# A linear-attention and mixture-of-experts kernel: quads of tiles, chunks of 64 tokens and transposed experts

## The chip, the cores and the metric

The kernel runs on one core of one Trainium2 chip. The metric is the device time of one execution in microseconds (us), as the median of several runs.

## What is computed

The input is 8 sequences of 1024 tokens with 128 features, float32.

```python
x = L0_attn_x
xn = _layernorm(x, axis=-1)
x = x + attention(xn) + experts(xn)
# attention: 16 heads of 8; k is layer-normed in each head; causal, linear (no softmax)
scores = jnp.where(causal, einsum('bthd,bshd->bhts', q_c, k_c), 0.0)
intra = einsum('bhts,bshd->bthd', scores, v_c); S = S + einsum('bthd,bthe->bhde', v_c, k_c)
# experts: 8, one for each token, the one with the largest affinity
assign = jnp.argmax(xn @ centroids.T, axis=1)
h = relu(einsum('etd,efd->etf', layernorm(xn) * ln_g + ln_b, w1) + b1)
y = xn + einsum('etf,edf->etd', h, w2) + b2
out = a * y + (1.0 - a) * xn          # a = sigmoid(xn . centroid)
```

The reference carries the state S from chunk to chunk of 64 tokens. Because nothing in the attention is nonlinear, any chunk length gives the same sum.

## The kernel before

A tile is 128 tokens; there are 64 tiles. A **quad** is four tiles of four sequences at the same place; there are 16 quads, and the quads of the two halves of the batch alternate. Every engine has a program of its own, in which the order of its work is written out by hand; semaphores hold the engines together. The program has three stages, one after the other.

- **Preparation** (`chunk`, 8 times; lines 1053 on for TensorE): tokens are loaded, layer-normed and transposed; affinities are computed; each expert's weights are loaded and transposed, with `ln_g` folded in; POOL adds the normed tokens to the residual and clears the slots in HBM. Then VectorE ranks all tokens by expert at once (lines 855 to 908).
- **Quads** (`quad`, 16 times). For each tile, `qk_trans` (L1096, L1098) transposes q and k, which were split into float16 parts; `scores` (L1108) makes, for each of four groups `g` of 32 rows, four products of 32 x 128 by 128 columns in float16. ScalarE copies half of the scores out of PSUM (L538) and POOL masks them (L343), VectorE masks the other half (L767). `weighted` (L1126) multiplies the scores by the values: 16 float32 products for each tile, with 128 x 32 weights and 128 columns. `inter` (L1118) adds the part of the state, `output` (L1134) applies W_o, `project` (L1065) makes q, k and v, `state_step` (L1139) updates the state. POOL also scatters each token's row to its slot in HBM (`scatter_rows`, L354).
- **Experts** (72 slots of 128 tokens in rounds of 8): `load_slots` reads a slot, `se_trans` (L1224) transposes it, `se_up` makes three products of 512 columns (L1232 to L1234, fp32r parts), VectorE adds the bias (L944), `se_hidden` (L1240) transposes the hidden layer, ScalarE applies relu (L605), `se_down` (L1248) makes four float32 products, VectorE adds b2 and scales (L952, L955), and POOL scatters the result into the output with an add (`scatter_out`, L410).

On TensorE a float32 product stands in the trace as two loads and two MATMUL records, a transpose or a float16 product as one of each.

## Time and profile before

| | |
|---|---|
| median of 3 runs | 767.69 us (765.97 to 768.08) |
| span of the profiled execution | 763.3 us; the median is 4.4 us above it |
| preparation, quads, experts | 85.5, 514.5, 163.3 us of the span |
| TensorE busy | 719.8 us (94%) |
| DVE, ACT, POOL busy | 387.7, 283.2, 329.9 us |

The page has a busy time for each engine, the span in 40 slices, the DMA queues, the chain of work that ended last and the costliest groups of instructions. The profiled execution has no other time of its own than its span. "L1126" is line 1126 of the kernel. PE is TensorE, PEld its weight loads, DVE is VectorE, ACT ScalarE, POOL GpSimd. Ends of matmuls are modelled, so the step from one start to the next tells the pace.

### The profile page before, as it was taken

Reading aid. Unit: us, or ns where it says so; the run is one execution under the profiler, and the core shown is the slowest. Engines: PE = TensorE matmul, PEld = TensorE weight load, DVE = VectorE, ACT = ScalarE, POOL = GpSimd, SP = SyncE. Lnnn points to the kernel's source line nnn. Section 1 sums busy time; section 2 is a strip of 40 time slices with the busy share of each in tenths; the row PEclk is TensorE's granted clock in tenths of the full one; section 3 lists DMA queues with packets and bytes.
Section 4 is the critical chain, followed back from the end, with each engine's and each line's share of the span. In section 5 each row is a group of like instructions: output and inputs, shape, how many; then the busy total and the mean of one; then the engine's idle time right before and its main releaser. Section 6 shows DMA issues by size and latency. Waiting matters only on the chain.

```text
span 763.3 us, 18096 instructions
## 1 busy us (share of the span) xinstructions
PE 719.8 (94%) x5828; PEld 568.7 (75%) x5830; DVE 387.7 (51%) x1080; ACT 283.2 (37%) x586; POOL 329.9 (43%) x361
## 2 busy tenths in 40 slices
PE   1896899999999999999999999999999899999994
PEld 1443677777777777777777777777777798899994
DVE  5978444343434434443344433444443577667773
ACT  1786233333333323323233233332433343434341
POOL 3553353333333333343333333333321277776776
PEclk9999699999999999999999999999999899999998
DMA  9791000000000000000000000000001154444451
GB/s 236 210 257 37 15 16 23 12 22 27 8 21 11 21 20 12 21 7 24 7 24 21 7 24 7 24 21 8 26 17 31 32 65 61 55 61 59 61 62 11
DMA packets 49807, 32.08 MB, mean 42 GB/s; under 512 B 8296, under 2 KB 46440, under 8 KB 49776
## 3 DMA queue, kind: packets, MB, share of 16 engines
q0 software_dynamic: 13840, 13.93, 10.7%
q1 hardware_dynamic: 32816, 17.73, 8.9%
q10 hardware_dynamic: 3120, 0.01, 0.2%
q8 instruction: 18, 0.29, 0.2%
q14 instruction: 13, 0.11, 0.1%
HBM read 14.07 MB, written 18.10 MB: 42 GB/s over the span
## 4 chain that ended last, share of the span: by engine, by line
PE 89%; DVE 3%; DMA 2%; issue 2%; SPq 1%; POOL 1%; ACT 1%; POOLq 0%; DVEq 0%; ACTq 0%
PE bank L1126 33%; PE bank L1108 11%; PE bank L1248 7%; PE bank L1065 7%; PE bank L1240 4%; PE bank L1118 4%; PE bank L1134 4%; PE bank L1096 3%; PE bank L1232 2%; PE bank L1234 2%; DMA resid<-in_L_attn_x_dram 2%; PE bank L1233 2%; PE bank L1139 2%; PE bank L1098 2%; PE bank L1060 1%
## 5 line engine op out<-in xcount | busy, mean ns | idle before, releaser
L1126 PE MATMUL bank<-pr,vz 128*32 128x128 f32 x2048 | 271.9, 276 | 0.0
L1126 PEld LDWEIGHTS bank<-pr,vz 128*32 128x32 f32 x2048 | 203.0, 110 | 27.9 <-issue 0.2
L343 POOL TENSOR_SCALAR_AFFINE_SELECT pr<-pr 128x512 f32<-128x512 f32 x128 | 81.4, 636 | 308.7 <-ACT pr L538 308.7
L767 DVE TENSOR_TENSOR pr<-bank,causal 128x512 f32<-128x512 f32 x128 | 88.0, 688 | 164.3 <-PE bank L1108 164.2
L410 POOL DMA_INDIRECT out_dram<-qs,idxe x72 | 112.3, 1559 | 58.7 <-DVE qs L955 32.3
L538 ACT ACTIVATE pr<-bank 128x512 f32<-128x512 f32 x128 | 76.3, 596 | 125.9 <-PE bank L1108 125.9
L1108 PE MATMUL bank<-qqt,kkt 32*128 32x128 f16 x1024 | 101.0, 218 | 1.6 <-DVE kkt L762 1.6
L762 DVE COPY kkt<-bank 128x512 f16<-128x512 f16 x64 | 27.2, 425 | 119.9 <-PE bank L1098 116.0
L1108 PEld LDWEIGHTS bank<-qqt,kkt 32*128 32x128 f16 x1024 | 56.9, 93 | 36.3 <-issue 15.3
L1248 PE MATMUL bank<-w2t,pr 128*128 x576 | 76.0, 275 | 0.0
L1248 PEld LDWEIGHTS bank<-w2t,pr 128*128 128x128 f32 x576 | 70.0, 192 | 6.4
L543 ACT ACTIVATE y<-bank 128x128 f32<-128x128 f32 x64 | 17.8, 277 | 152.3 <-PE bank L1126 150.0
L354 POOL DMA_INDIRECT slots_d<-xq,idxq x64 | 64.0, 999 | 22.3 <-POOL idxq L349 13.0
L944 DVE SCALAR_TENSOR_TENSOR pr<-bank,xs,b1b 128x512 f32<-128x512 f32 x72 | 54.1, 751 | 34.7 <-PE bank L1234 12.5
L605 ACT ACTIVATE pr<-bank 128x512 f32<-128x512 f32 x72 | 43.1, 598 | 72.3 <-PE bank L1240 48.7
L1065 PE MATMUL bank<-wqkv,xt 128*128 128x128 f32 x384 | 56.1, 290 | 0.7 <-ACT xt L501 0.7
L1065 PEld LDWEIGHTS bank<-wqkv,xt 128*128 128x128 f32 x384 | 47.2, 194 | 10.2 <-issue 9.1
L1240 PE MATMUL bank<-ident,pr 128*128 128x128 f32 x288 | 43.7, 275 | 0.0
L1096 PE MATMUL bank<-identh,qs 128*128 128x128 f16 x256 | 36.9, 224 | 5.1 <-DVE ks L757 5.1
L533 ACT ACTIVATE qqt<-bank 128x512 f16<-128x512 f16 x64 | 38.0, 593 | 8.0 <-PE bank L1098 7.7
L1232 PE MATMUL bank<-w1h,xse 128*128 x72 | 35.4, 491 | 2.3 <-DVE xse L938 2.0
L1096 PEld LDWEIGHTS bank<-identh,qs 128*128 128x128 f16 x256 | 23.7, 98 | 17.8 <-issue 17.8
(169 smaller groups left out, 931.0 us busy)
## 6 DMA issues: line engine op xcount, KB each, us to landing
slots_d<-zrow POOLq DMA_DIRECT2D x8, 594.0 KB, 6.6
xs<-slots_d SPq DMA_DIRECT2D x72, 66.0 KB
resid<-in_L_attn_x_dram SPq DMA_DIRECT2D x8, 512.0 KB, 6.6
out_dram<-res SPq DMA_DIRECT2D x16, 256.0 KB
state<-in_L_ffn_w_dram SPq DMA_DIRECT2D x8, 256.0 KB
res<-in_L_ffn_w_dram SPq DMA_DIRECT2D x8, 256.0 KB
out_dram<-qs,idxe POOLq DMA_INDIRECT x72
slots_d<-xq,idxq POOLq DMA_INDIRECT x64, 2.3
```

Source lines behind the costliest of these rows:

```text
L343: pool.affine_select(out=pr_v[:, g, :, :], in_=pr_v[:, g, :, :], compare_op=ALU.is_ge, fill=0.0, base=0, pattern=[[0, J], [1, P]], channel ...
L354: pool.indirect_dma_start(slots_d, bass.IndirectOffsetOnAxis(ap=idxq[:, half, i:i + 1], axis=0), xq[:, half, i, :], None, bounds_check=NS ...
L410: pool.indirect_dma_start(out_rows, bass.IndirectOffsetOnAxis(ap=idxe[:, a:a + 1].bitcast(U32), axis=0), ye[:, a, :], None, bounds_check=N ...
L538: nc.scalar.activation(pr[:, g, :], SC[0][:, :], ACT.Copy).then_inc(s("sc_even"), 1)
L767: nc.vector.tensor_tensor(pr_v[:, g, :, :], SC[1][:, :].rearrange("p (j t) -> p j t", j=J), bcast(causal[:, :], 1, J), ALU.mult)\
L944: nc.vector.scalar_tensor_tensor(out=hb[:, a % 2, :], in0=banks[a % 2][:, :], scalar=xs[:, a, D:D + 1], in1=b1b[:, e, :], op0=ALU.mult, op ...
L1065: last = mm(bank[:, i * P:(i + 1) * P], xt[:, i, :], wqkv[:, col:col + D], start=True, stop=True)
L1096: nc.tensor.transpose(qb16[:, j, :], qv, identh[:, :])
L1108: last = mm(SC[g % 2][:, j * P:(j + 1) * P], kkt[32 * g:32 * (g + 1), i % 2, j, :], qqt[32 * g:32 * (g + 1), i % 2, j, :], start=True, sto ...
L1126: last = mm(YB[32 * g:32 * (g + 1), 0:P], vz[:, i % 2, j, 32 * g:32 * (g + 1)], pr[:, g, j * P:(j + 1) * P], start=False, stop=(j == J - 1))
L1240: last = nc.tensor.transpose(banks[2 + a % 2][:, c * P:(c + 1) * P], hb[:, a % 2, c * P:(c + 1) * P], ident[:, :])
L1248: last = mm(banks[4 + a % 2][:, 0:D], ht[:, a % 2, c * P:(c + 1) * P], w2t[:, e, c, :], start=(c == 0), stop=(c == FC - 1))
```

## The change

Nearly every function is written anew, so the diff is cut to what the prediction speaks of. In words:

- **Chunks of 64.** Each tile is two chunks (`CH = 64`), with a state in the middle (`smid`). Scores beyond a chunk are not computed. A half-quad `h` is two tiles. `scores(h)` makes 32 float32 products with 32 rows, 64 columns of weights and 128 moving columns; successive ones lie on the four row groups, then on the other half of the columns. `products(h)` makes 32 with 128 rows, 32 columns of weights and 64 moving columns, successive ones on the four column groups. Transposes of q and k in float16 parts are gone: q and k are projected already transposed, with one product of 512 columns each, and ScalarE spreads q over masked copies (`q_expand`, four for each quad).
- **Masks.** VectorE masks the scores of three banks in one instruction of 1536 elements (of all four, 2048, from half-quad 18 on); ScalarE copies and POOL masks the fourth.
- **Layer norm, routing, ranking and scatters** run beside the quads, in four batches of 16 tiles. Scatters go straight from `rows`. Slots lie by expert at fixed places in HBM, so only the tails are cleared.
- **Experts' weights** are loaded and transposed in quads 7 to 14, on TensorE in the place of the token transposes.
- **Experts.** 71 slots. The hidden layer is computed transposed (four float32 products of 128 columns, relu with the bias on ScalarE), so that its transposes and the fp32r parts are gone. VectorE copies each slot's weights, 1024 elements, to one of three buffers. All is written out; no loop is left.

```diff
+    CH = 64
+    NC = P // CH
+    PAIRS = J // 2
...
-    def scores(m, i, g):
-        if g == 0:
-            pe.wait_ge(s("qq_sb"), m + 1)
-            pe.wait_ge(s("kk_sb"), m + 1)
-        reach(pe, s("pr_odd" if g % 2 else "sc_even"), 2 * m + g // 2)
-        for j in range(J):
-            last = mm(SC[g % 2][:, j * P:(j + 1) * P], kkt[32 * g:32 * (g + 1), i % 2, j, :],
-                      qqt[32 * g:32 * (g + 1), i % 2, j, :], start=True, stop=True)
-        last.then_inc(s("sc_ps"), 1)
...
-    def weighted(m, i, par, g):
-        if g == 0:
-            pe.wait_ge(s("vz_ready"), m + 1)
-        pe.wait_ge(s("pr_odd" if g % 2 else "pr_even"), 2 * m + g // 2 + 1)
-        for j in range(J):
-            last = mm(YB[32 * g:32 * (g + 1), 0:P], vz[:, i % 2, j, 32 * g:32 * (g + 1)],
-                      pr[:, g, j * P:(j + 1) * P], start=False, stop=(j == J - 1))
-        last.then_inc(s("av_ps"), 1)
...
+    def scores(h):
+        n = h // 2
+        if h % 2 == 0:
+            pe.wait_ge(s("kT_sb"), n + 1)
+            pe.wait_ge(s("qx_sb"), n + 1)
+        reach(pe, s("se_sb"), min(h, ROUTED))
+        reach(pe, s("so_sb"), h)
+        for b in range(PAIR):
+            i = h % 2 * PAIR + b
+            for c in range(NC):
+                tok = slice(i * P + CH * c, i * P + CH * (c + 1))
+                at = b * TW + c * PAIRS * CH
+                for up in range(2):
+                    for g in range(G):
+                        r = slice(SW * g, SW * (g + 1))
+                        last = mm(SC[g][CH * up:CH * (up + 1), at:at + PAIRS * CH],
+                                  kT[r, n % 2, tok], qx[r, n % 2, i, 2 * up:2 * up + 2, CH * c:CH * (c + 1)],
+                                  start=True, stop=True)
+        last.then_inc(s("sc_ps"), 1)
...
+    def products(h):
+        n = h // 2
+        half = n % 2
+        if h % 2 == 0:
...
+            i = h % 2 * PAIR + b
+            if b and h == NH - 1:
+                pe.wait_ge(s("so_sb"), NH + 1)
+            for c in range(NC):
+                for p in range(PAIRS):
+                    for g in range(G):
+                        k = b * TW + (c * PAIRS + p) * CH
+                        last = mm(Y[half][SW * g:SW * (g + 1), i * P + CH * c:i * P + CH * (c + 1)],
+                                  vz[:, half, c, i, g, p, :], pr[:, h % 2, g, k:k + CH],
+                                  start=(n < 2 and i == 0 and c == 0 and p == 0),
+                                  stop=(i == HALF - 1 and c == NC - 1 and p == PAIRS - 1))
+        last.then_inc(s("av_ps"), 1)
...
+            for a in range(P // GW):
+                for c, bank in ((0, Y[n % 2]), (1, FA))[:2 if n < NQ - 2 else 1]:
+                    r, k = slice(CH * c, CH * (c + 1)), slice(i * D + GW * a, i * D + GW * (a + 1))
+                    last = mm(bank[GW * a:GW * (a + 1), i * GW:(i + 1) * GW], kn[r, n % 2, k], vp[r, k], start=True,
+                              stop=True)
+        last.then_inc(s("ds_ps"), 1)
...
+    def q_project(n):
...
+        mm(FA[:, :], wqkv[:, 0:D], xT[:, HALF * n:HALF * (n + 1), :].rearrange("p i t -> p (i t)"), start=True,
+           stop=True).then_inc(s("q_ps"), 1)
...
+    for h in range(NH):
+        n = h // 2
+        more = n + 1 < NQ
+        norm = n + 1 < NCH
+        scores(h)
+        if h % 2 == 0:
+            if more:
+                kT_project(n + 1)
+            state_step(n)
+            if h:
+                products(h - 1)
+            inter_first(n)
+            if more:
+                k_transpose(n + 1)
+            if n and out_early(n):
+                output(n - 1)
+            if more:
+                q_project(n + 1)
+        else:
+            products(h - 1)
+            if n < 8 and n % 2 == 1:
+                affinities(n // 2)
+            if more:
+                v_project(n + 1, FB)
+            inter_second(n)
+            if n and not out_early(n):
+                output(n - 1)
+            if more:
+                pe.wait_ge(s("qT_sb"), n + 2)
+            if norm:
+                x_transpose(2 * n + 2, FA)
+            elif n - 7 < E:
+                w1_transpose(n - 7)
+            if more:
+                pe.wait_ge(s("v_sb"), n + 2)
+            if norm:
+                x_transpose(2 * n + 3, FB)
+            elif n - 7 < E:
+                w2_transpose(n - 7)
+            if n < 8 and n % 2 == 1:
+                affinities_back(n // 2)
+            if n == 0:
+                small_transpose()
...
+        for b in range(PAIR if h == NH - 1 else 1):
+            w = slice(b * TW, (b + 1) * TW) if h == NH - 1 else slice(0, PAIR * TW)
+            j = (w.stop - w.start) // CH
+            nc.vector.tensor_tensor(pr[:, h % 2, a:G, w].rearrange("p g (j t) -> p g j t", t=CH),
+                                    sc[:, a * BANK:G * BANK].rearrange("p (g w) -> p g w", w=BANK)[:, :, w]
+                                    .rearrange("p g (j t) -> p g j t", t=CH),
+                                    bcast(bcast(causal[:, :], 1, j), 1, G - a), ALU.mult).then_inc(s("so_sb"), 1)
...
+    def se_scale(k):
+        a = k % DEEP
+        dve.wait_ge(s(f"se_in{a}"), 16 * (k // DEEP + 1))
+        reach(dve, s("sex_ps"), k - 1)
+        nc.vector.tensor_scalar(xss[:, k % 2, :], xs[:, a, 0:D], xs[:, a, D:D + 1], None, ALU.mult)\
+            .then_inc(s("xss_ready"), 1)
+    def se_weights(k, e):
+        reach(dve, s("d_ps"), k - 2)
+        nc.vector.tensor_copy(ws[:, k % 3, :], wts[:, bass.ds(e * WE, WE)]).then_inc(s("ws_ready"), 1)
+    def se_shift(k, e):
+        a = k % DEEP
+        reach(dve, s("ye_ready"), k - 1)
+        dve.wait_ge(s("gates"), k // RING + 1)
+        nc.vector.scalar_tensor_tensor(out=yb[:, k % 2, :], in0=b2b[:, e, :], scalar=xs[:, a, D + 1:D + 2],
+                                       in1=xs[:, a, 0:D], op0=ALU.mult, op1=ALU.add).then_inc(s("yb_ready"), 1)
+    def se_result(k):
+        a = k % DEEP
+        reach(dve, s(f"out_done{a}"), 16 * (k // DEEP))
+        dve.wait_ge(s("yb_ready"), k + 1)
+        dve.wait_ge(s("d_ps"), k + 1)
+        nc.vector.scalar_tensor_tensor(out=ye[:, a, :], in0=banks[k % 2][:, 0:D],
+                                       scalar=xs[:, a, D + 1:D + 2], in1=yb[:, k % 2, :], op0=ALU.mult,
+                                       op1=ALU.add).then_inc(s("ye_ready"), 1)
...
+    def se_relu(k, e):
+        act.wait_ge(s("h_ps"), k + 1)
+        reach(act, s("d_ps"), k - 1)
+        for c in range(FC):
+            last = nc.scalar.activation(ht[:, k % 2, c * P:(c + 1) * P], inner(k)[:, c * P:(c + 1) * P],
+                                        ACT.Relu, bias=b1T[:, bass.ds(e * FC + c, 1)])
+        last.then_inc(s("ht_sb"), 1)
...
-    def se_bias(k, a, e):
-        dve.wait_ge(s("h_ps"), k + 1)
-        reach(dve, s("ht_ps"), k - 1)
-        nc.vector.scalar_tensor_tensor(out=hb[:, a % 2, :], in0=banks[a % 2][:, :], scalar=xs[:, a, D:D + 1],
-                                       in1=b1b[:, e, :], op0=ALU.mult, op1=ALU.add).then_inc(s("hb_ready"), 1)
-    def se_result(k, a, rnd, e):
-        reach(dve, s(f"out_done{a}"), 16 * rnd)
-        nc.vector.tensor_scalar(idxe[:, a:a + 1], xs[:, a, D + 2:D + 3], -1.0, float(NTOK), ALU.mult, ALU.add)
-        dve.wait_ge(s("ye_ps"), k + 1)
-        nc.vector.tensor_tensor(yb[:, a % 2, :], banks[4 + a % 2][:, 0:D], b2b[:, e, :], ALU.add)\
-            .then_inc(s("yb_done"), 1)
-        dve.wait_ge(s("yb_done"), k + 1)
-        nc.vector.tensor_scalar(ye[:, a, :], yb[:, a % 2, :], xs[:, a, D + 1:D + 2], None, ALU.mult)\
-            .then_inc(s("ye_ready"), 1)
-    def expert_round(i, e, first=False, last=False):
-        for a in range(RING):
...
+    def se_up(k):
+        pe.wait_ge(s("sex_sb"), k + 1)
+        pe.wait_ge(s("ws_ready"), k + 1)
+        reach(pe, s("ht_sb"), k - 1)
+        for c in range(FC):
+            last = mm(inner(k)[:, c * P:(c + 1) * P], ws[:, k % 3, c * P:(c + 1) * P], xsT[:, k % 2, :],
+                      start=True, stop=True)
+        last.then_inc(s("h_ps"), 1)
+    def se_down(k):
+        pe.wait_ge(s("ht_sb"), k + 1)
+        reach(pe, s("ye_ready"), k - 1)
+        for c in range(FC):
+            last = mm(banks[k % 2][:, 0:D], ht[:, k % 2, c * P:(c + 1) * P],
+                      ws[:, k % 3, F + c * D:F + (c + 1) * D], start=(c == 0), stop=(c == FC - 1))
+        last.then_inc(s("d_ps"), 1)
...
-    def se_up(k, a, e):
-        pe.wait_ge(s("sex_lo"), k + 1)
-        reach(pe, s("hb_ready"), k - 1)
-        h = banks[a % 2][:, :]
-        high, low = xse[:, a % 2, 0, :], xse[:, a % 2, 1, :]
-        mm(h, high, w1h[:, e, :], start=True, stop=False)
-        mm(h, high, w1l[:, e, :], start=False, stop=False)
-        mm(h, low, w1h[:, e, :], start=False, stop=True).then_inc(s("h_ps"), 1)
...
```

TensorE, one tile of a quad in the kernel before (`L1118` the state's part, `L1126` weighted, `L1108` scores, `L1134` output).

```order
L1118 MATMUL bank<-qt,state 128x128 [waits y_sb]
L1126 MATMUL bank<-pr,vz 32x128 [waits pr_even,vz_ready]
L1126 MATMUL bank<-pr,vz 32x128 x3
L1108 MATMUL bank<-qqt,kkt 128x128 [waits pr_odd]
L1108 MATMUL bank<-qqt,kkt 128x128 x3
L1126 MATMUL bank<-pr,vz 32x128 [waits pr_odd]
L1126 MATMUL bank<-pr,vz 32x128 x3
L1134 MATMUL bank<-wo,y 128x128 [waits y_sb]
L1108 MATMUL bank<-qqt,kkt 128x128 [waits sc_even,kk_sb,qq_sb]
L1108 MATMUL bank<-qqt,kkt 128x128 x3
L1126 MATMUL bank<-pr,vz 32x128 [waits pr_even]
L1126 MATMUL bank<-pr,vz 32x128 x3
```

The same engine in the changed kernel, the first half of a quad behind its scores and up to the next half's (`L1255` state, `L1328` products, `L1295` the state's part, `L1215` transposes of k, `L1337` output, `L1200` q, `L1274` scores).

```order
L1255 MATMUL bank<-vp,kn 64x64 x16
L1328 MATMUL bank<-pr,vz 32x64 [waits so_sb,pr_even]
L1328 MATMUL bank<-pr,vz 32x64 x31
L1295 MATMUL bank<-qT,state 64x64 [waits qT_sb,state_ready,dsta_sb]
L1295 MATMUL bank<-qT,state 64x64 x7
L1215 MATMUL bank<-ident,kT 128x128 [waits kT_sb]
L1215 MATMUL bank<-ident,kT 128x128 x3
L1337 MATMUL bank<-wo,y 128x128 [waits y_sb]
L1337 MATMUL bank<-wo,y 128x128 x3
L1200 MATMUL bank<-xT,wqkv 128x512 [waits rank_sb,dstb_sb]
L1274 MATMUL sc<-qx,kT 64x128 [waits so_sb,se_sb]
L1274 MATMUL sc<-qx,kT 64x128 x31
```

Scores and weighted products alternated in fours; each kind of product now stands in one run for a half-quad, and the shape changes between runs.

VectorE in the experts, one slot before and one after (each from its bias or scale on).

```order
L944 ISA [waits ht_ps,h_ps]
L944 SCALAR_TENSOR_TENSOR pr<-bank,xs,b1b 128x512
L950 TENSOR_SCALAR idxe<-xs 128x1 [waits out_done3]
L952 ISA [waits ye_ps]
L952 TENSOR_TENSOR yb<-bank,b2b 128x128
L955 TENSOR_SCALAR qs<-yb,xs 128x128 [waits yb_done]
```

```order
L1009 TENSOR_SCALAR wide<-rows 128x128 [waits sex_ps,se_in4]
L1022 ISA [waits gates,ye_ready]
L1022 SCALAR_TENSOR_TENSOR qx<-b2b,rows 128x128
L1030 SCALAR_TENSOR_TENSOR qx<-bank,rows,qx 128x128 [waits d_ps,yb_ready,out_done0]
L1015 ISA [waits d_ps]
L1015 COPY tokens<-xT 128x1024
```

The instruction of 512 elements is gone and one copy of 1024 elements has come, with waits on TensorE's `d_ps` ahead of it.

## Rows read from the trace of the kernel before

**Rows 1.** Page, part 1: busy time by engine
```profile
PE 719.8 (94%) x5828; PEld 568.7 (75%) x5830; DVE 387.7 (51%) x1080; ACT 283.2 (37%) x586; POOL 329.9 (43%) x361
```

**Rows 2.** Busy time by stage: us, then PE, PEld, DVE, ACT, POOL busy, PEclk, DMA share, GB/s
```profile
0.00:85.50 85.50, 55.46 (x279) 30.79 (x282) 65.21 (x308) 48.51 (x92) 36.45 (x41) 0.94 0.63 165
85.50:600.00 514.50, 511.01 (x4415) 398.57 (x4415) 211.99 (x418) 173.26 (x356) 181.15 (x248) 0.99 0.06 18
600.00:763.30 163.30, 153.30 (x1137) 139.34 (x1136) 110.56 (x354) 61.44 (x140) 112.27 (x72) 0.98 0.42 53
```

**Rows 3.** TensorE timeline (start us, us, what), pieces of one quad
```profile
300.65 1.16 PE L1139 MATMUL bank<-kv 128*128 128x128 f32 x8
301.74 0.39 PE L1108 MATMUL bank<-qqt,kkt 32*128 32x128 f16 x4
302.06 1.06 PE L1126 MATMUL bank<-pr,vz 128*32 128x128 f32 x8
303.06 0.23 PE L1096 MATMUL bank<-identh,qs 128*128 128x128 f16 x1
303.12 0.22 PE L1098 MATMUL bank<-identh,ks 128*128 128x128 f16 x1
```

**Rows 4.** TensorE timeline, end of the last quad: two column groups in a row
```profile
589.62 1.53 PE L1126 MATMUL bank<-pr,vz 128*32 128x128 f32 x16
```

**Rows 5.** TensorE and its weight loads: 512-column products, two at once
```profile
58.12 1.02 PE L1037 MATMUL bank<-xt,qs 128*128 128x512 f32 x2
59.08 1.12 PE L1038 MATMUL bank<-dstate,ones 1*128 1x512 f32 x2
60.13 1.05 PE L1012 MATMUL bank<-vz,cen_t 128*32 128x512 f32 x4
...
60.12 0.14 PEld L1012 LDWEIGHTS bank<-vz,cen_t 128*32 128x32 f32 x4 [0.76 <-ACT vz L443]
```

**Rows 6.** Chain of waits, one expert tile (start us, us, what)
```profile
649.97 0.89 PE bank L1248 x8
650.86 0.44 PE bank L1240 x4
651.30 0.24 PE bank L1232
...
652.00 0.11 PE bank L1224
652.11 0.89 PE bank L1248 x8
```

**Rows 7.** POOL timeline: scatters back to back
```profile
741.92 1.56 POOL L410 DMA_INDIRECT out_dram<-qs,idxe  x1 [0.30 <-issue]
743.78 1.56 POOL L410 DMA_INDIRECT out_dram<-qs,idxe  x1 [0.30 <-issue]
```

**Rows 8.** Groups by line (busy us, mean ns, then idle before)
```profile
L767 DVE TENSOR_TENSOR pr<-bank,causal 128x512 f32<-128x512 f32 x128 | 88.0, 688 | 164.3 <-PE bank L1108 164.2
...
L538 ACT ACTIVATE pr<-bank 128x512 f32<-128x512 f32 x128 | 76.3, 596 | 125.9 <-PE bank L1108 125.9
...
L952 DVE TENSOR_TENSOR yb<-bank,b2b 128x128 f32<-128x128 f32 x72 | 20.8, 289 | 10.3 <-PE bank L1248 9.1 <-issue 1.0
...
L543 ACT ACTIVATE y<-bank 128x128 f32<-128x128 f32 x64 | 17.8, 277 | 152.3 <-PE bank L1126 150.0 <-issue 2.3
L386 POOL TENSOR_TENSOR state<-state,dstate 128x512 f32<-128x512 f32 x14 | 17.7, 1268 | 0.1
...
L727 DVE COPY xq<-rows 128x528 f32 x12 | 5.1, 422 | 0.0
```

**Rows 9.** Timeline: first tokens' statistics, and VectorE beside a scatter
```profile
7.47 1.64 DVE L665 BATCH_NORM_STATS2 stats<-resid 128x6 f32<-128x128 f32 x8 [1.04 <-DMA resid<-in_L_attn_x_dram]
...
744.26 0.61 DVE L955 TENSOR_SCALAR qs<-yb,xs 128x128 f32<-128x128 f32 x1
```

**Rows 10.** Timeline: TensorE's last products
```profile
751.56 2.06 PE L1248 MATMUL bank<-w2t,pr 128*128 x16
```

1785 lines of the change are left out of this document (927 added, 858 removed).

## The prediction

> **What bounds the kernel now.** I read the page first: TensorE is busy 94% of the span, the others half of it or less [rows 1]. Then the busy time by stage: 85.5 us of preparation, 514.5 us of quads with TensorE busy for 511.0, and 163.3 us of experts with TensorE busy for 153.3, its granted clock at 0.94 to 0.99 of 2.4 GHz [rows 2]. A quad takes 514.5 / 16 = 32.2 us. So three questions decide: does the preparation go under the quads, what does a quad cost on TensorE, and does an expert's slot get shorter. The fourth, whether another engine takes over, comes with each.
>
> TensorE's timeline of a quad gives the prices. Starts are what counts: four weighted products go from 302.06 to 303.06, 1.00 us; four scores take 0.32 (from 301.74), four full float32 products 1.09 (from 300.65) [rows 3]. In the expert stage, where no shape changes, four float32 products take 0.89, four transposes 0.44 and one 0.11 [rows 6]. Against 0.89, weighted and full products cost 0.11 and 0.20 more among the quads, so I put a change of the tile's shape at 0.15, and a float32 product of 128 columns lasts 0.89 / 4 = 0.22 us on its tile, whatever its weights are. One of 512 columns takes 59.08 - 58.12 = 0.96 [rows 5].
>
> Two rows show that products on different column groups run at once. Two products of 512 columns on 32 columns of weights each, four records, take 1.05 us where one with 128 columns of weights takes 1.02 [rows 5]. At the end of the last quad, eight weighted products on two groups take 1.53 us where four take 1.06 [rows 3, 4].
>
> **The change, part by part.** A sum for the changed kernel, stage by stage, against 763.3 us.
>
> *Start.* The first tokens' statistics begin at 7.47 us [rows 9]; W_qkv was loaded ahead of them and now is loaded behind, and the first half is fetched alone, so 6 us. Statistics of four tiles (8 take 1.64), moments, root, norm, transposes, two copies, q and the spreading of q [rows 6, 8, 9] are some nine steps of about 1 us: first scores at **15 us**, not 85.5. Zeroing of slots and residual adds are gone; loads of weights lie beside the quads.
>
> *A quad on TensorE.* Large parts: q and k, 2 x 0.96 = 1.92; transposes of k 0.44; v 0.89; output 0.89; eight transposes of tokens or of experts' weights 0.88 [rows 5, 6]; affinities, in four quads 1.05 and 0.44, 0.37 in the mean; some eleven changes of shape at 0.15, 1.65. Together **7.04 us**.
>
> Small parts: 64 scores products, 64 weighted ones and in the mean 30 for the state (480 in all), 158. Each is two loads and two records, 632 instructions. By the array alone they are short: the scores lie on eight tiles, 64 x 0.22 / 8 = 1.8 us; a product of 64 columns lasts half of 0.22, so 64 x 0.11 / 4 = 1.8; the state's go two at a time, 30 x 0.11 / 2 = 1.7. That is 5.3 us. But nothing in the trace shows 632 instructions issued in that time. The densest long run, the transposes of q and k, starts a load and a product each 0.06 us, 0.03 for an instruction (0.028 by the array's 128 columns at 2.4 GHz and a few ns) [rows 3], and that is the array's own pace for it; a burst of four loads is over in 0.14 us with the last one's own length in it [rows 5], so they start at most 0.035 apart and, if a load itself lasts some 0.1, 0.01 apart. The price of an issued instruction thus lies between 0.010 and 0.028, or below where the array's 5.3 us decide. I take 0.015, nearer to the burst, since the other end is not limited by issue at all: 632 x 0.015 = **9.5 us**. Bounds: 5.3 (the array) and 632 x 0.028 = 17.7.
>
> So a quad is 16.5 us on TensorE, and 12.3 to 24.7 by the bounds. 16 x 16.5 = **264 us**.
>
> The Trainium skill ("TensorE: Matmul & The Clock Gate", on the gap of 56 ns) says that starts of matmuls never come closer than about 25 ns, however few columns they have. By it the 316 records of a quad would take 7.9 us and no quad could cost less than 14.9. The trace's four records in 1.05 us are too few to tell.
>
> *A quad elsewhere.* VectorE: 128 elements take 0.289 and 512 take 0.688 [rows 8], 1.04 ns for an element, so a mask of 1536 takes 1.76 and one of 2048 2.3. Two masks 3.5, k's variance, the scaling of v and the result 0.69 each, a reciprocal 0.5, two state masks of 256 0.84, statistics 1.64 [rows 9] and moments 0.7, norm 0.6, a share of the routing 2.3 (eight short operations of 0.29): 12.2 us, and 10 to 11 in the late quads. ScalarE: four spreads, two score copies and seven other copies of 0.6 [rows 8] and 1.5 of small ones, 9.3. POOL: two masks and two state sums at 1.27 for 512 elements [rows 8], 3.8, three scatters of at most 1.56 [rows 7], norms and values 1.7, 10.2. All lie under TensorE's 16.5, the nearest being VectorE. If the small products ran at the array's pace, VectorE and TensorE would meet at 12 to 13 us, and waits between them would make it 13. The scores' four banks are single: scores wait for the mask of the half-quad ahead, 2 us from the end of that one's scores, and TensorE has over 5 us of other work in between. Routing, which stood ahead of the quads, is spread over quads 1 to 9, in VectorE's slack; without that slack it would show with its 2.3 us.
>
> *Between quads and experts.* The first slots are read during the last quad. The last copy, output and first hidden layer leave **3 us**.
>
> *Experts.* TensorE for a slot before: 0.89 for the second layer, 0.44 for the transposes, 0.70 for the first layer (651.30 to 652.00), 0.11: 2.14 [rows 6]. Now: two groups of four products and one transpose, 0.89 + 0.89 + 0.11 = 1.89. POOL's scatters follow each other at 1.86 (741.92 to 743.78) [rows 7], which no change touches. ScalarE's five copies of 0.28 are 1.4; VectorE's copy of 1024 elements is at most 0.422 x 1024 / 528 = 0.82, with three short ones of 0.29 1.7 [rows 8]. With four engines at 1.4 to 1.9, I take 2.0 for a slot: 71 x 2.0 = **142 us** (136 if TensorE alone paces it). So the gain here is small: taking 0.44 of transposes away moves the bound only to POOL.
>
> *End.* From the start of the last two slots' products (751.56, 1.8 us of work) to the end of the span were 11.7 us [rows 10], some 2 of them a backlog of scatters (one scatter each 1.86, one slot's products each 2.14 or less); **8 us** from the last products on.
>
> Sum: 15 + 264 + 3 + 142 + 8 = 432, plus the 4.4 us that the runs' median stands above the profiled span: **436 us**.
>
> **The rivals.**
>
> *A. Issue paces the small products at 0.028 us.* For it: no row shows a longer run at a faster pace [rows 3]. Against it: that pace is also that of the array for 128 columns. The quad is 24.7 us, the sum 16 x 8.2 = 131 us more, 567 us. Chance 0.10.
>
> *B. VectorE and POOL shut each other out in the experts.* In the trace a VectorE operation that takes 0.29 alone took 0.61 while a scatter ran that had begun at 743.78 [rows 7, 9], so one holds up the other. The change puts a copy of 0.82 in each slot beside a scatter. Fully exclusive, a slot is 1.86 + 0.82 + 0.29 = 2.97: 71 x 0.97 = 69 us more, 505 us. Against it: scatters kept their 1.56 us beside all of VectorE's operations [rows 7]. Chance 0.10. The Trainium skill ("SBUF — State Buffer", "SBUF: two separate sides") states this as a lock for the whole instruction, which such a copy takes against POOL's descriptors; by that rule this rival would be the forecast. The 0.61 agrees in kind, the unchanged 1.56 doesn't.
>
> *C. Every small product pays the change of tile.* Slower than before. A step to another row or column group would cost what a change of shape costs now, 0.13 of the 0.11 to 0.20 above: scores 64 x 0.35 = 22.4, weighted 64 x 0.24 = 15.4, state 30 x 0.24 = 7.2, plus 7.04 = 52 us for a quad, 16 x 35.5 = 568 us more, 1004 us. It would be slower than before from 37.2 us for a quad on, that is 0.19 us for a small product, where I take 0.06. Against it stand both rows that show two groups at once [rows 4, 5]. Only row groups are not shown there. Chance 0.03.
>
> *D. The ring of waits.* A quad passes from TensorE to ScalarE and VectorE and back some ten times. If a quarter of it were waiting, 20 us for a quad, 492 us. Chance 0.06. That the change does not do what it says isn't in question: 71 slots and 158 small products stand in its order of instructions.
>
> **How the numbers follow.** The forecast has 0.71, and is the likeliest. Its own range goes from 13 us a quad with 136 us of experts, 374 us (little likely, since all must go well; I set 385), to 18 us a quad, 460. To hold eight in ten I take in B and D, up to 520. Every case but C is faster by far more than the 0.3% that a measurement of this kernel can tell from no change: faster 0.96, same 0.01, slower 0.03.
>
> **What would show it.** Right: first scores near 15 us; 32 scores products within about 2 us and 32 weighted ones within 2 us of TensorE's timeline; quads of 16 to 17 us with TensorE over 85% busy; slots at 1.9 to 2.0 us, TensorE and POOL both near full. Wrong: quads of 12 to 13 with VectorE at 90% (then issue costs nothing); 32 scores in 3.5 us (A); scatters longer than 1.56, or VectorE's copy longer than 0.82 in the expert stage (B); a TensorE that waits for ScalarE or VectorE for more than 2 us of a quad (D).

## The result, and the profile after

The changed kernel takes **365.75 us** (median of 5 runs, 365.05 to 366.98), the kernel before 768.08 us beside it (5 runs, 765.97 to 768.74): a ratio of 0.476, with a 95% interval of 0.475 to 0.478. I had forecast 436 us with a range of 385 to 520. Faster was right, and so was the mechanism; the size was not, and the time lies 19 us below the range.

The page of the changed kernel, its busy times, slices of TensorE's clock and instruction queue, beside [rows 1]:

```profile
span 363.3 us, 17565 instructions
...
PE 342.1 (94%) x6868; PEld 293.0 (81%) x6868; DVE 287.1 (79%) x799; ACT 241.8 (67%) x657; POOL 251.7 (69%) x245
...
PEclk9989999999999999999999999999999999999996
...
q8 instruction: 55, 0.90, 1.1%
```

TensorE is as full as before, with half the time. Busy time by stage, in place of the three stages of [rows 2] (start and length, then PE, PEld, DVE, ACT, POOL busy, granted clock, DMA share, GB/s):

```profile
0.00:13.00 13.00, 9.58 (x62) 7.77 (x62) 10.23 (x76) 6.84 (x14) 4.83 (x21) 1.00 0.64 183
13.00:217.00 204.00, 195.52 (x5599) 149.44 (x5598) 169.91 (x443) 140.69 (x280) 133.94 (x153) 0.99 0.36 104
218.00:350.00 132.00, 131.52 (x1175) 130.88 (x1174) 103.02 (x274) 90.62 (x354) 105.16 (x67) 1.00 0.53 71
```

The spans differ by 763.3 - 363.3 = 400.0 us. Of these, preparation gave 85.5 - 13.0 = 72.5, the quads 514.5 - 204.0 = 310.5, and experts with end and seam 163.3 - 146.3 = 17.0. A quad is 204.0 / 16 = 12.75 us, in place of 32.2. TensorE's timeline of one late quad (start, us, what, how many; the step from one start to the next tells the pace):

```profile
156.94 1.27 PE L1274 MATMUL sc<-qx,kT 32*64 32x128 f32 x64
158.25 1.12 PE L1209 MATMUL bank<-xT,wqkv 128*128 128x512 f32 x2
159.30 0.69 PE L1255 MATMUL bank<-vp,kn 64*64 64x64 f32 x32
160.32 1.10 PE L1328 MATMUL bank<-pr,vz 128*32 128x64 f32 x64 [0.32 <-issue]
161.35 0.68 PE L1295 MATMUL bank<-qT,state 64*64 64x64 f32 x16
161.96 0.65 PE L1215 MATMUL bank<-ident,kT 128*128 128x128 f32 x4
162.45 1.02 PE L1200 MATMUL bank<-xT,wqkv 128*128 128x512 f32 x2
163.41 1.39 PE L1274 MATMUL sc<-qx,kT 32*64 32x128 f32 x64
164.72 1.10 PE L1328 MATMUL bank<-pr,vz 128*32 128x64 f32 x64
165.75 1.16 PE L1222 MATMUL bank<-wqkv,xT 128*128 128x128 f32 x8
166.84 0.68 PE L1306 MATMUL bank<-qT,smid 64*64 64x64 f32 x16
167.45 1.16 PE L1337 MATMUL bank<-wo,y 128*128 128x128 f32 x8
168.45 0.60 PE L1228 MATMUL bank<-ident,w1raw 128*128 128x128 f32 x4
168.89 0.63 PE L1233 MATMUL bank<-ident,w2raw 128*128 128x128 f32 x4
169.48 0.82 PE L1274 MATMUL sc<-qx,kT 32*64 32x128 f32 x37
```

Read it in two parts. The 64 records of `products` (L1328), which with their loads are 128 instructions, go from 164.72 to 165.75: 1.03 us, 8 ns an instruction. The scores' 64 (L1274) take 1.31, and 1.19 in the median of the 32 runs. All small products of this quad, scores, products and state, take 1.31 + 1.02 + 1.03 + 0.61 + 1.31 + 1.03 + 0.61 = 6.9 us with a gap of 0.32; the large parts the other 5.6. The sum is the quad's 12.54 us.

The experts, TensorE and then POOL over the same stretch, which answer to [rows 6, 7]:

```profile
278.71 0.27 PE L1414 MATMUL sc<-ident,wide 128*128 128x128 f32 x1
278.82 1.06 PE L1429 MATMUL bank<-tokens,qx 128*128 128x128 f32 x8
279.72 1.06 PE L1421 MATMUL sc<-wide,tokens 128*128 128x128 f32 x8
280.61 0.27 PE L1414 MATMUL sc<-ident,wide 128*128 128x128 f32 x1
```

```profile
278.09 1.55 POOL L494 DMA_INDIRECT out_dram<-qx,rows  x1 [0.30 <-issue]
279.94 1.55 POOL L494 DMA_INDIRECT out_dram<-qx,rows  x1 [0.30 <-issue]
281.80 1.60 POOL L494 DMA_INDIRECT out_dram<-qx,rows  x1 [0.30 <-issue]
```

A slot is 280.61 - 278.71 = 1.90 us, back to back on TensorE, and POOL's scatters follow at 1.85 to 1.86 here, with nothing between them but their 0.30; over the stage most steps are 1.85 to 1.93. Groups by line (busy, mean ns of one, idle time before):

```profile
L494 POOL DMA_INDIRECT out_dram<-qx,rows x71 | 112.9, 1590 | 35.1 <-issue 22.1
...
L856 DVE TENSOR_TENSOR pr<-sc,causal 128x1536 f32<-128x1536 f32 (+2 forms) x33 | 63.6, 1929 | 17.4 <-PE sc L1274 17.2
...
L1015 DVE COPY tokens<-xT 128x1024 f32 x71 | 55.2, 778 | 0.0
L1274 PEld LDWEIGHTS sc<-qx,kT 32*64 32x64 f32 x2048 | 32.5, 132 | 16.4 <-issue 15.8
```

And the end of the timeline, the last slot's second layer and POOL's last scatter, beside [rows 10]:

```profile
354.03 1.16 PE L1429 MATMUL bank<-tokens,qx 128*128 128x128 f32 x8 [0.43 <-ACT qx L694]
...
357.38 1.55 POOL L494 DMA_INDIRECT out_dram<-qx,rows  x1 [0.30 <-issue]
```

### The profile page after: what moved, and what is told of

It reads as the page before. It is cut to its first block, busy times and chain, and to the rows that moved or that the text cites. A ratio compares the mean times of both kernels' runs of the same rounds, so it can differ in the third digit from the quotient of the medians.

```text
span 363.3 us, 17565 instructions
## 1 busy us (share of the span) xinstructions
PE 342.1 (94%) x6868; PEld 293.0 (81%) x6868; DVE 287.1 (79%) x799; ACT 241.8 (67%) x657; POOL 251.7 (69%) x245
## 3 DMA queue, kind: packets, MB, share of 16 engines
q0 software_dynamic: 12272, 8.54, 17.2%
## 4 chain that ended last, share of the span: by engine, by line
issue 25%; POOL 13%; PE 11%; DVE 1%; DMA 1%; POOLq 1%; ACT 1%; SPq 0%; DVEq 0%; ACTq 0%
POOL out_dram L494 13%; PE bank L1328 2%; PE sc L1274 2%; PE bank L1337 2%; PE bank L1222 1%; DMA out_dram<-res 1%; POOLq L71 1%; PE bank L1200 1%; PE bank L1306 1%; DVE pr L856 1%; PE bank L1209 1%; PE bank L1295 1%; PE bank L1255 1%; PE bank L1215 0%; PE bank L1233 0%
## 5 line engine op out<-in xcount | busy, mean ns | idle before, releaser
L494 POOL DMA_INDIRECT out_dram<-qx,rows x71 | 112.9, 1590 | 35.1 <-issue 22.1
L694 ACT ACTIVATE qx<-sc,b1T 128x128 f32<-128x128 f32 x280 | 79.8, 368 | 39.6 <-PE sc L1421 39.6
L420 POOL DMA_INDIRECT slots_d<-rows,pos_i x64 | 64.2, 1003 | 43.1 <-issue 11.0
L856 DVE TENSOR_TENSOR pr<-sc,causal 128x1536 f32<-128x1536 f32 (+2 forms) x33 | 63.6, 1929 | 17.4 <-PE sc L1274 17.2
L1429 PE MATMUL bank<-tokens,qx 128*128 128x128 f32 x568 | 75.3, 276 | 0.8 <-ACT qx L694 0.7
L1421 PE MATMUL sc<-wide,tokens 128*128 128x128 f32 x560 | 74.0, 275 | 0.2 <-issue 0.2
L1429 PEld LDWEIGHTS bank<-tokens,qx 128*128 128x128 f32 x568 | 69.0, 192 | 1.4 <-ACT qx L694 1.4
L1421 PEld LDWEIGHTS sc<-wide,tokens 128*128 128x128 f32 x560 | 68.1, 192 | 0.3 <-issue 0.3
L1015 DVE COPY tokens<-xT 128x1024 f32 x71 | 55.2, 778 | 0.0
L1274 PEld LDWEIGHTS sc<-qx,kT 32*64 32x64 f32 x2048 | 32.5, 132 | 16.4 <-issue 15.8
L1274 PE MATMUL sc<-qx,kT 32*64 32x128 f32 x2048 | 40.6, 282 | 1.2 <-DVE pr L856 1.2
L1328 PE MATMUL bank<-pr,vz 128*32 128x64 f32 x2048 | 38.0, 221 | 3.0 <-issue 3.0
L1328 PEld LDWEIGHTS bank<-pr,vz 128*32 128x32 f32 x2048 | 31.6, 110 | 8.2 <-issue 6.9
L1222 PEld LDWEIGHTS bank<-wqkv,xT 128*128 128x128 f32 x128 | 15.5, 191 | 4.4 <-issue 3.4
```

Source lines behind the costliest of these rows:

```text
L420: pool.indirect_dma_start(slots_d, bass.IndirectOffsetOnAxis(ap=pos_i[:, t:t + 1], axis=0), rows[:, t, :], None, bounds_check=E * RT * P - ...
L494: pool.indirect_dma_start(out_rows, bass.IndirectOffsetOnAxis(ap=xs[:, a, D + 2:D + 3].bitcast(U32), axis=0), ye[:, a, :], None, bounds_ch ...
L694: last = nc.scalar.activation(ht[:, k % 2, c * P:(c + 1) * P], inner(k)[:, c * P:(c + 1) * P], ACT.Relu, bias=b1T[:, bass.ds(e * FC + c, 1)])
L856: nc.vector.tensor_tensor(pr[:, h % 2, a:G, w].rearrange("p g (j t) -> p g j t", t=CH), sc[:, a * BANK:G * BANK].rearrange("p (g w) -> p g ...
L1015: nc.vector.tensor_copy(ws[:, k % 3, :], wts[:, bass.ds(e * WE, WE)]).then_inc(s("ws_ready"), 1)
L1274: last = mm(SC[g][CH * up:CH * (up + 1), at:at + PAIRS * CH], kT[r, n % 2, tok], qx[r, n % 2, i, 2 * up:2 * up + 2, CH * c:CH * (c + 1)], ...
```

## The experiments

Each number is the median of its own runs; the kernel before was run beside each (765.7 to 767.0 us), and the changed kernel's 365.75 is the mark for the rest.

**1. One part of the change alone, in the kernel before.** `weighted_pair` issues the eight records of `weighted` on one column group and the eight of the next in turns, after both groups' scores. Nothing is made smaller or left out.

```diff
-                        weighted(m - 1, i_b, par_b, 2)
-                        weighted(m - 1, i_b, par_b, 3)
+                        weighted_pair(m - 1, i_b, par_b, 2)
...
-                    weighted(m, i, half, 0)
-                    weighted(m, i, half, 1)
+                    weighted_pair(m, i, half, 0)
```

> The kernel before, with one thing of the change alone: the eight small products of each of two column groups (0 and 1, then 2 and 3) are issued in turns, after both groups' scores, instead of all eight of one group and then all eight of the next. The instructions are the same and as many. Theory 1 (products on different tiles of the array run at once, and that is most of what the change gained): a pair of groups takes 4 passes x 2 rounds x 8 products of 64 columns... that is about half of the time that its two runs of eight took, 1.0 to 1.2 us less for each pair, two pairs a tile, 64 tiles: 100 to 150 us less than before, so 615 to 665 us, if no other engine turns out to be the bound in between. Rival (the gain comes from the order of the stages, and TensorE takes the products one after the other whatever their tiles): within 0.5 per cent of before, 764 to 772 us.

It took 649.33 us (646.93 to 650.75; ratio 0.847, 0.844 to 0.850), 118 us less. TensorE's timeline:

```profile
300.17 1.07 PE L1137 MATMUL bank<-pr,vz 128*32 128x128 f32 x16
301.17 0.49 PE L1146 MATMUL bank<-wo,y 128*128 128x128 f32 x2
```

Sixteen records take the 1.00 us that eight took in [rows 3]. 128 pairs at 0.99 us are 127 us; 118 came. TensorE now waits ahead of the scores for VectorE's mask in 15 places, 6.7 us in all, a wait that the kernel before does not have.

**2. The same for all four column groups:** one run of 32 records for a tile, in turns over four groups, after the next tile's first two scores.

> The kernel before, with the small products of all four column groups of a tile issued in turns, one run of 32 records in the place of four runs of 8, after the next tile's first two scores; nothing else. With pairs alone 16 records took 1.00 us where 8 had taken 0.99, and the kernel 649 us. Theory 1 (the array's pace on each tile decides, up to four groups at once, and an instruction costs no more than 1.0 / 64 = 0.016 us): 32 records take 1.0 to 1.1 us, so 1 us less for a tile than with pairs, 64 us less, 585 us; with waits, since a tile's copies and masks can no longer begin before the last tile's products are all done, 575 to 620 us. Theory 2 (issue costs 0.03 us an instruction, the densest pace that the trace of before shows): 32 records take 2 us and the time stays at 645 to 660 us.

606.26 us (606.12 to 606.92; ratio 0.791, 0.790 to 0.793), 161 us less than before.

```profile
300.52 1.08 PE L1136 MATMUL bank<-pr,vz 128*32 128x128 f32 x32
301.53 0.66 PE L1060 MATMUL bank<-ident,xq 128*128 128x128 f32 x4
```

32 records, 1.01 us: 8, 16 and 32 records cost the same. By this step alone 64 us should have gone beyond the pairs; 43 did, inside the 575 to 620 us that I expected. The products gave 55 of the 64: their steps sum to 73.6 us, with pairs to 128.4. Waits took 12 back, as expected: the trace has TensorE waiting ahead of the scores for ScalarE (5.0 us) and VectorE (3.1), and ahead of the products for POOL's mask (3.2) and for nothing that it shows (4.0). The granted clock was 0.95 over the quads, where it was 0.99 before, which cost a part that no run separates from the waits.

**3. The same part undone in the changed kernel:** `products` goes through the column groups one after the other. **4.** The same for the row groups in `scores`, where successive products still change between the two column halves. The lines are of the third.

```diff
-                    for c in range(NC):
-                        for p in range(PAIRS):
-                            for g in range(G):
+                    for g in range(G):
+                        for c in range(NC):
+                            for p in range(PAIRS):
```

> The weighted products of a half-quad in another order: the eight of one column group one after another, instead of going round the four groups. Same products, same loads, same count of instructions. Theory 1 (products on different column groups run at once, and TensorE sets the pace of the quads): a half-quad's 32 take 32 x 0.112 + 0.13 = 3.7 us from start to next start instead of 1.03, so 2.7 us more for each of 32, about 85 us more in all, 451 us. Theory 2 (the pace of small products is that of issuing them, whatever tile they lie on): no change, 366 us.

> The scores of a half-quad in another order: all eight of one row group, then the next row group; successive ones still alternate between the two column halves. Same products, same count. Theory 1 (row groups run at once like column groups, eight tiles in all): only two run at once now, 32 x 0.22 / 2 + 0.13 = 3.6 us instead of 1.31, 32 x 2.3 = 74 us more, 440 us. Theory 2 (row groups don't run at once, only column halves do): no change; the 1.31 us of now would then not be explained.

393.55 us (ratio to before 0.514, 0.513 to 0.515), 27.8 more, and 396.86 (0.518, 0.517 to 0.520), 31.1 more. The first fence is of the third experiment, the second of the fourth:

```profile
164.57 2.41 PE L1328 MATMUL bank<-pr,vz 128*32 128x64 f32 x64
166.91 0.68 PE L1295 MATMUL bank<-qT,state 64*64 64x64 f32 x16
```

```profile
163.07 2.59 PE L1274 MATMUL sc<-qx,kT 32*64 32x128 f32 x64
165.59 1.12 PE L1209 MATMUL bank<-xT,wqkv 128*128 128x512 f32 x2
```

Products take 2.34 us where they took 1.03, scores 2.52 where they took 1.19. Both kinds of group run at once. My 3.7 and 3.6 us, and with them the expected 451 and 440 us, were too high. In the serial run of the products the first and last records start 56 ns apart, and those between mostly 25 to 30. I read this as the next group's first products starting before this one's last are through, so that even a serial order overlaps at its seams.

By these steps, 32 half-quads would lose 32 x 1.31 = 42 us and 32 x 1.33 = 43; 14 and 12 us fewer were lost. In experiment 3 the products' steps sum to 74.2 us, 34.4 more than the changed kernel's 39.8, whose mean is longer than 1.03, and the scores' are 2.0 shorter (37.5 for 39.5). In experiment 4 the scores' steps sum to 81.5, 42.0 more, and the products' are 6.5 shorter (33.3 for 39.8). TensorE's idle time from the first scores to the first hidden layer is 8.5 us in the changed kernel, 2.3 and 2.7 in these two. So about half of what was not lost is waiting that is gone; experiment 6 shows what part of it was for.

**5. The order of two neighbouring scores** on the row groups and column halves is exchanged (`up` inside `g`).

> The scores go to the two column halves of a row group one after another and then to the next row group, instead of all row groups of one half first. The same eight tiles. Theory 1 (what counts is that eight tiles are busy; the 0.3 us above the array's 0.87 plus 0.13 are loads or issue, which don't change): no change within 2 us. Rival (the 0.3 us come from loads that go to tiles of the same columns one after another): 0.3 us less for each of 32 half-quads, 10 us less, 356 us.

365.55 us (362.75 to 366.01), the same. Scores took 1.14 us for a half-quad in the median instead of 1.19. The 10 us that the rival promised did not come.

**6. Each product of `products` is split in two of 32 columns.** The same work for the array, 256 instructions in place of 128 for a half-quad.

```diff
+                                for z in range(0, CH, CH // 2):
+                                    at = i * P + CH * c + z
-                                last = mm(Y[half][..., i * P + CH * c:i * P + CH * (c + 1)], ..., pr[:, h % 2, g, k:k + CH],
+                                    last = mm(Y[half][..., at:at + CH // 2], ..., pr[:, h % 2, g, k + z:k + z + CH // 2],
```

> Each weighted product is split in two of 32 columns with the same weights: 64 products, 256 instructions for a half-quad, the same columns in all. Theory 1 (an instruction of a small product costs at most the 8 ns that the 128 of now need, 1.03 us / 128): 256 x 0.008 = 2.1 us at most instead of 1.03, or 1.1 us if issue is cheaper still: 2 to 35 us more, 368 to 401 us. Rival (no two matmul records start closer than about 25 ns): 128 records x 0.025 = 3.2 us, 2.2 us more for each of 32, 70 us more, 436 us. Rival A of the prediction (0.015 to 0.028 for an instruction): 3.8 to 7.2 us, 90 to 195 us more.

422.45 us (420.07 to 423.18; ratio 0.551, 0.549 to 0.554), 56.7 more. That is more than the 401 us at most of the first theory and less than the rivals' 436 and more. Two runs of its products, an undisturbed one and another, with what follows each, the busy times and granted clock of two stretches, and its instruction queue:

```profile
163.88 1.48 PE L1330 MATMUL bank<-pr,vz 128*32 128x32 f32 x128
165.29 0.56 PE L1295 MATMUL bank<-qT,state 64*64 64x64 f32 x12
167.68 0.33 PE L1295 MATMUL bank<-qT,state 64*64 64x64 f32 x4 [1.83 <-issue]
...
184.74 1.00 PE L1330 MATMUL bank<-pr,vz 128*32 128x32 f32 x78
187.64 0.95 PE L1330 MATMUL bank<-pr,vz 128*32 128x32 f32 x50 [1.90 <-issue]
188.51 2.08 PE L1222 MATMUL bank<-wqkv,xT 128*128 128x128 f32 x8
...
13.00:277.00 264.00, 223.29 (x7667) 175.07 (x7667) 170.71 (x447) 141.86 (x282) 133.85 (x153) 0.95 0.29 84
188.50:190.60 2.10, 2.10 (x14) 1.86 (x12) 0.00 (x0) 0.00 (x0) 0.00 (x0) 0.50 0.04 8
...
q8 instruction: 71, 1.16, 1.2%
```

Undisturbed, 256 instructions take 165.29 - 163.88 = 1.41 us, **5.5 ns each**, 11 ns for a record with its load. That is the lowest price of issue that any row here shows. But over the run TensorE stands still for 26.6 us ahead of its products, in 20 gaps of up to 2.4 us, where nothing that the profile shows holds it; the changed kernel has 3.0 in 7. What grew with the instructions is the instruction queue: 71 packets in place of 55 (18 before, where loops repeat the same code), 0.26 MB more for 4096 more instructions, 64 bytes each, so that a packet of 16 KB holds 256.

The kept traces hold the time of every packet, and they settle what the gaps wait for. Ahead of all its work in this run's quads, TensorE has 30 such gaps, 37.6 us in all. Counted over TensorE's own instructions, every one of the 30 stands at the same place in a block of 256 (the 193rd or 194th), and every one ends 1.2 to 1.6 us after a packet of this queue has landed. So do all seven ahead of the products of the changed kernel. TensorE had run out of instructions. No run changes the supply alone, but 30 gaps of 30 at one place in 256, each behind a landing, leave little room for another cause. In none of the runs of the changed kernel and its variants do two packets start less than 3.2 us apart between 13 and 280 us; by that, an estimate of the fastest lasting pace is 3.2 / 256 = 0.0125 us an instruction.

So a second price stands behind the first: short bursts go at 5.5 ns an instruction, but the supply doesn't keep that up. In the changed kernel the same gaps are there, in small, and they are what experiments 3 and 4, with longer work between the same instructions, had less of: one gap of this kind in the two together.

Where the 57 us went: TensorE stands still for 40.4 us of the quads in place of 8.5, so 32 us; an undisturbed run of products is 0.38 us longer, 12 us for 32; and the granted clock is 0.95 in place of 0.99. In six stretches of the quads it is at the lower of its two levels, 1.2 GHz, each right behind a gap of 1.6 to 2.4 us, though not behind every such gap. There the eight records of L1222 take 2.01 us from start to start, with 0.50 granted, where they take 1.09 at 2.4 GHz. By the difference the clock has the remaining 13 us or so; no run tests it alone.

**7. and 8. Which engine has slack.** VectorE gets a reduction of 0.54 us ahead of each half-quad's mask, or TensorE gets four idle transposes ahead of each half-quad's scores, 0.53 us from start to start with the change of shape. The first two lines are the one, the last the other.

```diff
+                nc.vector.tensor_reduce(out=scr[:, h, :], in_=wqkv[:, :].rearrange("p (h d) -> p h d", d=DK), axis=AX,
+                                        op=ALU.add)
...
+                keep_busy(4)
```

> One more VectorE instruction ahead of each half-quad's mask: a sum over 384 elements into a place that nobody reads, about 0.55 us, 32 of them, 18 us of VectorE in all. Theory 1 (TensorE paces the quads, VectorE has some 2 us of slack in each): at most a third of it shows, 0 to 6 us more, 366 to 372 us. Rival (VectorE, the other engine near full, sets the pace through the masks): all of it shows, 18 us more, 384 us.

> Four more transposes on TensorE ahead of each half-quad's scores, into the scores' own bank before they are overwritten: 4 x 0.11 = 0.44 us and perhaps a change of shape, 32 of them, 14 to 19 us in all. Theory 1 (TensorE paces the quads): nearly all of it shows, 12 to 19 us more, 378 to 385 us. Rival (VectorE or the ring of waits does): a third or less, up to 371 us.

369.11 us (368.79 to 370.29): 17.2 us of VectorE work cost 3.4. And 376.18 us (375.98 to 377.02): 17.5 us of TensorE work cost 10.4, just less than the 12 of the first theory and more than its rival allows. TensorE paces the quads for the most part, with VectorE behind it.

**9. The experts without VectorE's copy of weights** from slot 3 on (later slots then work on other experts' weights). **10. The experts with a lighter TensorE:** the second layer has three products of four, so a quarter of it is left out. The first three lines are the one, the last two the other.

```diff
+                w = WE if k < 3 else 1
-                nc.vector.tensor_copy(ws[:, k % 3, :], wts[:, bass.ds(e * WE, WE)])
+                nc.vector.tensor_copy(ws[:, k % 3, 0:w], wts[:, bass.ds(e * WE, w)])
...
-                for c in range(FC):
+                for c in range(FC - 1):
```

> From slot 3 on VectorE copies one element instead of the slot's 1024 weights, so that the experts after the first three slots work on weights of others: that part of the result is left out. Theory 1 (TensorE paces a slot at 1.89 us): no change, 366 us, and scatters stay at 1.56 to 1.6 us. Rival B of the prediction (VectorE's copy and POOL shut each other out): scatters shorter than 1.59 in the mean, steps of POOL shorter, VectorE's other operations back at 0.28; with TensorE as the pace the time would still fall by no more than 3 us.

> The second layer leaves out a quarter of the hidden features (three products instead of four): TensorE needs 1.67 us for a slot instead of 1.89. Theory 1a (POOL's scatters at 1.86 us come right behind TensorE as the bound): 71 x 0.03 = 2 us less, 364 us, slots at 1.86. Theory 1b (TensorE alone counts): 71 x 0.22 = 16 us less, 350 us. Rival (ScalarE, with 1.14 for relu, 0.29 for the transposed tokens and its waits, is next): slots between 1.67 and 1.86.

Without the copy 364.65 us (364.14 to 365.86; ratio 0.476, 0.475 to 0.477), which can't be told from the changed kernel's 0.476; but the mean scatter takes 1550 ns where it took 1590. With three products 369.81 us (368.54 to 371.19; ratio 0.483, 0.481 to 0.484): **less work, 4 us more**, where I had expected 350 to 364. Its POOL timeline and TensorE's:

```profile
283.00 1.67 POOL L494 DMA_INDIRECT out_dram<-qx,rows  x1 [0.30 <-issue]
284.98 2.36 POOL L494 DMA_INDIRECT out_dram<-qx,rows  x1 [0.30 <-issue]
287.65 1.63 POOL L494 DMA_INDIRECT out_dram<-qx,rows  x1 [0.30 <-issue]
```

```profile
276.92 1.42 PE L1429 MATMUL bank<-tokens,qx 128*128 128x128 f32 x6 [2.56 <-ACT qx L694]
```

Beside the scatter at 284.98 VectorE ran two copies (at 284.91 and 286.58), and it took 2.36 us. Over the whole stage the 11 scatters with two copies beside them took 1.71 to 2.40 us, the 49 with one 1.55 to 1.75. A longer scatter also meets a second copy more easily, so this alone doesn't say which makes which.

**11. Both together**, to see whether the copy makes the long scatters.

> Two earlier experiments together: from slot 3 on VectorE does not copy the expert's weights, and the second layer leaves out a quarter of the hidden features. Left out of the computation: both of these. With the second alone TensorE had 1.67 us of work for a slot, yet the kernel took 4 us longer than the changed one: one scatter in eight took 1.8 to 2.4 us, and TensorE waited 1.3 to 2.6 us behind it. Theory 1 (VectorE's copy does it: where it comes at a bad moment of POOL's work on a scatter, the scatter is longer by about the copy's 0.7 us): no scatter over 1.8 us, slots at POOL's 1.86 us, TensorE waits evenly; 71 x 0.04 us less than the changed kernel, 360 to 364 us. Theory 2 (it is the DMA queue or its ring, or an earlier part of the chain, and not the copy): the long scatters and the waits stay, 367 to 371 us.

360.89 us (360.12 to 362.68; ratio 0.471, 0.470 to 0.472), inside the 360 to 364 of the first theory, and POOL's timeline is even:

```profile
281.25 1.55 POOL L494 DMA_INDIRECT out_dram<-qx,rows  x1 [0.30 <-DVE qx L1031]
283.10 1.55 POOL L494 DMA_INDIRECT out_dram<-qx,rows  x1 [0.30 <-issue]
284.95 1.55 POOL L494 DMA_INDIRECT out_dram<-qx,rows  x1 [0.30 <-issue]
```

No scatter of the stage takes over 1.63 us; most follow at 1.85. The copy was the cause of the long ones. TensorE still waits for ScalarE ahead of the second layer, in seven gaps of up to 2.8 us, 9.1 in all. POOL's 1.85 now paces the slots: with a quarter of the second layer gone the whole kernel gains only 4.9 us.

## Why the prediction was wrong

The sum again, against the profile, both to the span. The slots are counted from their first hidden layer (218.70) up to the start of the last slot's second layer (354.03), and the end from there:

| part | forecast | measured | difference |
|---|---|---|---|
| to the first scores | 15 | 13.0 | -2.0 |
| 16 quads | 264 | 204.0 | -60.0 |
| seam | 3 | 1.7 | -1.3 |
| 71 slots | 142 | 135.3 | -6.7 |
| end | 8 | 9.3 | +1.3 |
| span | 432 | 363.3 | -68.7 |

**The step that failed is the price of an issued instruction.** I had bounded it between 0.010 and 0.028 us, "or below where the array's 5.3 us decide", and taken 0.015: 9.5 us for a quad's 632 instructions. The timeline shows 6.9 - 0.3 = 6.6 us, 0.0104 each, and experiment 6 shows that issue is not even what limits them: a burst goes at 0.0055. I had the array's bound (5.3) worked out from rows and let a guess about issue override it. That is 2.9 us for each quad, 46 us in 16.

**Changes of the tile's shape were the second.** I counted eleven at 0.15 us, 1.65. The large parts of the late quad take 5.6 us where their pure work is 5.0 (1.92 + 0.44 + 0.89 + 0.89 + 0.88), so 0.6 for all: the values' products (L1222, 1.09 to the next start) pay 0.20 and the output's (L1337) 0.11, as [rows 3] had it, but of the two wide ones the first (L1209, 1.05) pays 0.09 and the second (L1200, 0.96) nothing. With the quad's affinities left out of my 7.04, that is 1.1 us a quad, 17 us. (The 6.6 us of the small parts hold their own changes of shape, some of my eleven, so the split between the two steps is rough; their sum, 63 us, is not.) I had multiplied a price of single cases by a count of places that I hadn't seen.

Waits, which the sum had at nothing, gave 8.5 us back: TensorE is busy for 195.5 of the quads' 204.0 us, where it was for 511.0 of 514.5 [rows 2]. Of these 8.5, 3.0 are gaps in the supply of instructions (experiment 6), a cost that no part of the prediction had. The affinities, 6 us in my sum, are the rest of the 60: the late quad has none, and yet the quads' mean busy time, 195.5 / 16 = 12.2 us, is no longer than its own.

**Slots.** I took 2.0 us "with four engines at 1.4 to 1.9"; TensorE's own 1.89 held, for 6.7 us in all. My margin was for engines that might hinder each other; they do so in experiment 10, but hardly in the changed kernel, where POOL is 0.04 us behind. The 4.4 us between span and median, which I took from the kernel before, were 2.5.

**The range.** I had written the right case down: small products at the array's pace, VectorE and TensorE meeting at 12 to 13 us, 13 for a quad, 374 us. I called it little likely and cut the range at 385. Quads of 12.75 and a quicker start make it 365.75. The sign that I had named for being wrong, quads of 12 to 13 us with VectorE at 90%, came true in its first half; VectorE is at 83% (169.9 of 204.0).

**What was right.** The direction. That products on different column groups run at once, read from two rows [rows 4, 5], and that row groups do too, which no row showed and experiment 4 bears out. VectorE in the quads 169.9 / 16 = 10.6 us (forecast 12.2, late quads 10 to 11), ScalarE 8.8 (9.3), POOL 8.4 (10.2), all below TensorE. POOL's scatters at 1.85 to 1.93 (1.86). Removing the transposes of the experts moves the bound only to POOL.

**The rivals.** A (issue at 0.028) and C (each small product pays a change of tile) are excluded by 64 records in 1.03 us; even with its products in series (experiment 3) the changed kernel takes half the time of before. D (a ring of waits) is worth under 0.6 us a quad. B (VectorE and POOL exclude each other) is real and small in the changed kernel. Both signs that I had named are there: the mean scatter takes 1.59 us, and 20 of 71 copies took more than 0.82, up to 1.03. But it costs 0.04 us for a mean scatter, and experiment 9 without the copy is no faster that the runs can tell. It shows clearly only in experiment 10, where two copies meet one scatter and the scatter is longer by up to 0.8 us (2.36 to 1.55), more than one copy's 0.68. The Trainium skill ("SBUF — State Buffer", "SBUF: two separate sides") has a lock for the whole instruction. Of the 67 scatters that had a whole copy beside them, 36 took under 1.60 us, and all but five of the others at most 1.63: a copy of 0.68 us inside a scatter of 1.55 shows no such thing. The other rule that I had weighed, of the Trainium skill too ("TensorE: Matmul & The Clock Gate", "Wait — 56ns, not 53.3ns?"), that starts of matmuls are never nearer than some 25 ns, would have made a quad 14.9 us at least. The quads take 12.75, with records 1.03 / 64 = 16 ns apart in the mean in the changed kernel and 11 ns in experiment 6. It does not hold between records on different tiles.

**Where the 400 us came from.** In the quads, `weighted` was 16 runs of 0.99 us a quad, 254 us in all, and `products` has 39.8: 214 of the 310 us. A product there also has half the columns that one of `weighted` had. Experiment 2 shows 161 us of it in the old kernel without any other part. Scores went from 256 x 0.32 = 82 to 39.5, 42 us, in which half as many scores and another type (float32 for float16) are mixed with the order. The rest, 54 us, I put down to transposes of q and k that are gone and to wide projections; no run takes it apart.

## What to carry to other kernels

Before anything else, look at whether consecutive small products on TensorE go to the same 32-row or 32-column group. Eight, sixteen and thirty-two records in turns over one, two and four groups cost the same 1.0 us here, so in this kernel the loop over groups belongs innermost; that reordering alone took 21% off the old kernel. When you bound the cost of many small instructions, take the array's pace as the forecast if two rows show overlap, and keep the issue price for the upper end, but count instructions: they came in blocks of 256, never less than 3.2 us apart, so that over some hundreds in a row their supply was a bound of its own. Splitting a product in two cost 57 us for no more work on the array.

## What the runs showed of the hardware that I had not expected

- An instruction of TensorE can cost 5.5 ns (256 in 1.41 us), but the same 256 took up to 4.2 us where the supply ran dry, with gaps of up to 2.4 us. Each such gap stood at the same place of a block of 256 instructions and ended 1.2 to 1.6 us after a packet of the instruction queue had landed.
- Column groups in series overlap at their seams: 2.34 us for four groups in a row, where one at a time they would take 3.7 by my price of 0.112 a product.
- Less work made a kernel slower: three products in place of four, 4 us more, since VectorE's copies of weights made some of POOL's scatters longer (2.36 us in place of 1.55, with two copies beside it). With the copy gone too, the same kernel was 4.9 us faster than the changed one.
